# Sums of weight magnitudes moved between engines at the start of a gated block kernel, with a new order around up's mean

## The reference

```
def weight_quant(w):
    scale = 1.0 / clip(mean(abs(w)), EPS, None)
    q = clip(round(w * scale), -1.0, 1.0) / scale
def act_quant(x):
    scale = 127.0 / clip(max(abs(x), axis=-1), EPS, None)
    q = clip(round(x * scale), -128.0, 127.0) / scale
x = x + tanh(g_xattn) * mlstm(layernorm(x), ctx, ctx, ...)
y = layernorm(x)
g, u = act_quant(y) @ weight_quant(w_gate).T, act_quant(y) @ weight_quant(w_up).T
h = square(relu(g)) * u
x = x + tanh(g_ffn) * (act_quant(h) @ weight_quant(w_down).T)
```

## Time and profile before

| | |
|---|---|
| median of 3 runs | 606.54 us (606.44 to 607.38) |
| the profiled execution | 606.26 us, of it span 604.5 us |
| TensorE products busy | 579.7 us, 96% |
| VectorE busy | 529.8 us, 88% |
| ScalarE busy | 449.5 us, 74% |
| GpSimd busy | 125.8 us, 21% |
| DMA | 62.68 MB, 104 GB/s mean |

### The profile page before, as it was taken

How to read it: one execution, slowest core, us unless ns; L and a number is a source line. 1 busy time by engine, 2 the same in 40 slices (tenths; PEclk the granted TensorE clock), 3 DMA queues, 4 the chain that set the end, 5 groups by cost and what they waited for, 6 DMA issues and landing times.

```text
span 604.5 us, 18405 instructions
## 1 busy us (share of the span) xinstructions
PE 579.7 (96%) x6584; PEld 340.3 (56%) x6584; DVE 529.8 (88%) x1152; ACT 449.5 (74%) x922; POOL 125.8 (21%) x284
## 2 busy tenths in 40 slices
PE   8997779999999999999999999999999999999996
PEld 4744445656565565656565565656565565656452
DVE  3899998998989898998989898998989899897964
ACT  4789779687786868687786868687686868687662
POOL 3255052120121212020121212031121212021100
PEclk9999879999999999999999999999999999999999
DMA  8958132050504114060503205050502305030000
GB/s 304 383 199 300 46 122 72 21 193 2 195 17 142 67 38 171 3 206 0 192 17 120 90 23 186 0 209 0 188 21 91 118 18 192 3 106 1 20 36 35
DMA packets 44113, 62.68 MB, mean 104 GB/s; under 512 B 1848, under 2 KB 25648, under 8 KB 44080
## 3 DMA queue, kind: packets, MB, share of 16 engines
q1 hardware_dynamic: 44080, 62.24, 29.3%
HBM read 53.72 MB, written 8.51 MB: 103 GB/s over the span
## 4 chain that ended last, share of the span: by engine, by line
PE 77%; DVE 8%; ACT 6%; issue 5%; POOL 2%; DMA 1%; DVEq 0%; SPq 0%; ACTq 0%; POOLq 0%
PE yb L1230 16%; PE gb L1204 16%; PE ub L1204 16%; PE tp L1251 8%; PE ab L1238 7%; PE ab L1218 4%; PE tp L1278 3%; PE ab L1261 2%; PE ab L1239 2%; POOL stage L446 2%; DVE stage L806 1%; PE ab L1312 1%; ACT wgT L535 1%; ACT wdT L535 1%; DMA xs<-in_x 1%
## 5 line engine op out<-in xcount | busy, mean ns | idle before, releaser
L1204 PE MATMUL gb<-wgT,xqT 128*128 128x512 bf16 x512 | 133.5, 384 | 0.1
L1204 PE MATMUL ub<-wuT,xqT 128*128 128x512 bf16 x512 | 132.8, 382 | 0.6 <-DVE stage L806 0.5
L1230 PE MATMUL yb<-wdT,stage 128*128 128x512 bf16 x512 | 120.6, 380 | 1.8 <-ACT stage L557 1.8
L543 ACT ACTIVATE relu<-gb 128x512 f32<-128x512 f32 x128 | 75.1, 587 | 45.9 <-PE gb L1204 45.6
L806 DVE TENSOR_TENSOR stage<-relu,ub 128x512 f32<-128x512 f32 x128 | 86.8, 678 | 15.4 <-ACT relu L545 14.5
L1204 PEld LDWEIGHTS ub<-wuT,xqT 128*128 128x128 bf16 x512 | 49.7, 99 | 64.0 <-DVE stage L806 5.4
L545 ACT ACTIVATE relu<-relu 128x512 f32<-128x512 f32 x128 | 80.8, 631 | 4.1
L933 DVE SCALAR_TENSOR_TENSOR dmat<-ab,dmat 128x384 f32<-128x384 f32 x128 | 65.0, 548 | 19.0 <-POOL dmat L454 13.5
L1230 PEld LDWEIGHTS yb<-wdT,stage 128*128 128x128 bf16 x512 | 47.1, 98 | 49.9 <-ACT stage L557 1.1
L1204 PEld LDWEIGHTS gb<-wgT,xqT 128*128 128x128 bf16 x512 | 46.1, 101 | 45.1 <-issue 1.3
L454 POOL TENSOR_SCALAR_AFFINE_SELECT dmat<-dmat 128x256 f32<-128x256 f32 x128 | 55.4, 461 | 62.9 <-ACT dmat L603 50.4
(11 more groups left out here) (131 smaller groups left out, 896.4 us busy)
## 6 DMA issues: line engine op xcount, KB each, us to landing
dmat<-max_rows SPq DMA_DIRECT2D x15, 1024.0 KB, 5.0
values<-in_ctx_v SPq DMA_DIRECT2D x16, 520.0 KB, 7.6
xs<-in_x SPq DMA_DIRECT2D x16, 512.0 KB, 5.8
cT<-in_ctx_t SPq DMA_DIRECT2D x16, 512.0 KB, 6.9
out<-stage SPq DMA_DIRECT2D x32, 256.0 KB, 2.0
stage<-in_w_gate SPq DMA_DIRECT2D x4, 1024.0 KB, 12.8
stage<-in_w_up SPq DMA_DIRECT2D x4, 1024.0 KB, 13.8
stage<-in_w_down SPq DMA_DIRECT2D x4, 1024.0 KB, 7.1
```

Source lines behind the costliest of these rows:

```text
L543: nc.scalar.activation(relu[:, c % 2, :], gb[c % 2][:, :], ACT.Relu).then_inc(g_free, 1)
L1204: last = nc.tensor.matmul(bank[c % 2][:, :], xqT[par][:, t, d, :], w[:, d, c * CH:(c + 1) * CH], start=(d == 0), stop=(d == KD - 1))
L1230: done = nc.tensor.matmul(yb[:, :], hqT[:, c, :], wdT[:, c, :], start=(c == 0), stop=(c == KF - 1))
```

## The change

- The sum of piece 1 of up and that of piece 2 of down go from VectorE to ScalarE.
- The sum of piece 3 of down is made from the identity |w| = 2 max(w, 0) - w. GpSimd writes max(w, 0) of the piece into the second half of wdT (four operations of 128 x 512). TensorE multiplies the piece by a constant -4/128 and the positive part by 2 x 4/128, each as four products with 32 stationary columns and 512 moving ones, whose results go to four groups of 32 rows of yb. VectorE then sums the 512 columns of yb into asum. This adds waits: TensorE on GpSimd's four operations, VectorE on TensorE's products.
- In VectorE's prologue log_forget(1) and cumulative(1,1) go behind scale_heads and the residuals, the token statistics ahead of the running maximum, and quantise_tokens(0) ahead of weight_scale(1), the mean of up.
- GpSimd waits for the token statistics between the scalings of pieces 0 and 1 of gate.
- ScalarE takes the sum of piece 3 of up after tokens_rstd; it takes the sign of piece 1 of gate after those of piece 0 of up, and that of piece 2 in step 0 after the first relu and square.
- TensorE's keep_warm counts around weight_total(1) are 6, 5 and 8 in place of 12 and 20.

The diff, cut to its core:

```
 gpsimd
+            nc.gpsimd.memset(twice[:, :], 2 * KD / P).then_inc(positive_done, 1)
+            nc.gpsimd.memset(minus[:, :], -KD / P).then_inc(positive_done, 1)
...
             scale_weight(0, 0)
+            gp.wait_ge(ln2_step, 4)
             scale_weight(0, 1)
...
                     token_factor(0, 0)
+                    gp.wait_ge(w_in[2][3], 16)
+                    for k in range(KD):
+                        part = slice(CH * k, CH * (k + 1))
+                        nc.gpsimd.tensor_scalar(positive[:, part], weight_piece(2, 3)[:, part], 0.0, 0.0,
+                                                ALU.max, ALU.add).then_inc(positive_done, 1)
                     scale_weight(2, 0)
 scalar
-            magnitudes(1, 2, 3)
-            magnitudes(1, 3, 4)
+            magnitudes(1, 1, 3)
+            magnitudes(1, 2, 4)
             tokens_rstd(0)
+            magnitudes(1, 3, 5)
             sign_weight(0, 0)
-            sign_weight(0, 1)
-            sign_weight(1, 0)
             quantise_second(0)
             tokens(0, 0)
-            sign_weight(0, 2)
+            sign_weight(1, 0)
+            sign_weight(0, 1)
             exponentials(1, 0, 1)
...
                 relu_square(b, 0, 0)
                 if third:
+                    sign_weight(0, 2)
                     exponentials(n, 1, npar)
...
                 relu_square(b, 0, 3)
+                if third:
+                    magnitudes(2, 2, 8)
 vector
             gates_in(1)
-            magnitudes(1, 1)
-            log_forget(1)
             dve.wait_ge(tanh_done, 1)
             scale_heads(0)
-            cumulative(1, 1)
+            log_forget(1)
             residual(0, 0)
             second_residual(0, 0)
+            cumulative(1, 1)
+            token_stats(0, 0)
             dve.wait_ge(rows_spread, NP)
             running_max(1, 1)
-            token_stats(0, 0)
             token_centres(0, 0)
+            quantise_tokens(0)
             weight_scale(1)
...
             scale_weight(1, 0)
-            dve.wait_ge(winv_step, WINV[1] + 2)
-            quantise_tokens(0)
...
-                if not prev:
-                    magnitudes(2, 2)
                 hidden(b, 0, 2)
...
                 hidden_max(b, 0, 0)
+                hidden(b, 0, 3)
                 if not prev:
-                    magnitudes(2, 3)
-                hidden(b, 0, 3)
+                    dve.wait_ge(columns_done, 1)
+                    nc.vector.tensor_reduce(asum[:, 2, 3:4], yb[:, :], axis=AX_X, op=ALU.add).then_inc(asum_done[0], 1)
 tensor
+            def column_sums():
+
+                pe.wait_ge(positive_done, 2 + KD)
+                pe.wait_ge(winv_step, WSUM[1])
+                for weights, src, first in ((minus, weight_piece(2, 3), True), (twice, positive, False)):
+                    for k in range(KD):
+                        rows = slice(P // KD * k, P // KD * (k + 1))
+                        done = nc.tensor.matmul(yb[rows, :], weights[:, :], src[:, CH * k:CH * (k + 1)], start=first, stop=not first)
+                done.then_inc(columns_done, 1)
...
             max_columns(1)
-            keep_warm(12, ub[1])
+            keep_warm(6, ub[1])
             weight_total(1)
-            keep_warm(20, ub[1])
+            keep_warm(5, ub[1])
             token_columns(0)
+            keep_warm(8, ub[1])
...
                 chunk(b, 0, 3, par)
+                if not prev:
+                    column_sums()
                 if n is not None:
                     heads_out(n, 2, npar)
```

More of the change, by code:

```diff
@@ L82, in gated_block @@
         asum = sb("asum", [P, 3, 4], F32)
+        twice = sb("twice", [P, P // KD], F32)
+        minus = sb("minus", [P, P // KD], F32)
+        positive = wdT[:, :, :].rearrange("p k d -> p (k d)").bitcast(F32)[:, FF:2 * FF]
         wmean = sb("wmean", [P, 3], F32)
@@ L168, in gated_block @@
         total_done = sem("total_done")
+        positive_done = sem("positive_done")
+        columns_done = sem("columns_done")
         winv_step = sem("winv_step")
@@ L711, in step @@
                 else:
-                    magnitudes(2, 0, 5)
+                    magnitudes(2, 0, 6)
                 relu_square(b, 0, 2)
@@ L717, in step @@
                 if third:
-                    magnitudes(2, 1, 6)
+                    magnitudes(2, 1, 7)
                 relu_square(b, 0, 3)
+                if third:
+                    magnitudes(2, 2, 8)
                 if n is not None:
@@ L1180, in weight_total @@
             def weight_total(m):
-                pe.wait_ge(asum_done[0], (2, 3, 5)[m])
-                pe.wait_ge(asum_done[1], (2, 5, 7)[m])
+                pe.wait_ge(asum_done[0], (2, 2, 3)[m])
+                pe.wait_ge(asum_done[1], (2, 6, 9)[m])
                 if m > 0:
```

## The result

The changed kernel took 609.68 us (median of 5 runs, 609.35 to 609.91) against 606.54 (605.65 to 607.38): a ratio of 1.0056, 95% interval 1.004 to 1.0072. **It is slower, by 3.1 us between the medians and by 3.4 us (0.56%) by the ratio**, and outside the range of the prediction (604.5 to 607.9). The span of the profiled execution grew from 604.5 to 608.1.

The account below looks back on a forecast made before the run. TensorE, busy for 96% of the span, bounds from about 94 us; before that, down's mean on VectorE decides. The mean comes 0.4 us earlier: 606.54 - 0.4 = 606.1 us, range 604.5 to 607.9.

Parts of the forecast that it names:

- The relay and its start: Before down's mean: ScalarE's last sign of gate ends at 57.1, piece 3 lands at 62.3, GpSimd waits for it.
- GpSimd's four operations: Positive parts of down's piece 3 on GpSimd: 3.2 to 4.2 us, taken as 3.65, ending at 66.0.
- The column sums: TensorE's products for down's piece 3: 1.9 us at full clock, 3.6 at half, the 32-wide groups overlapping.
- The slower rival: TensorE's column groups do not overlap: C 72.8 and 610.1 us in series, 608.4 overlapped in twos; chance 0.14.
- C: End of TensorE's column_sums: 67.9 at full clock, 69.6 at half, mostly near 68.8.
- The clock: TensorE, idle 2 to 3.6 us before column_sums, runs most of it at 1.2 GHz: 3.6 us.
- C + 6.7: Down's mean is ready 6.7 us after C, through heads_out and VectorE's normaliser; break-even is C = 69.2.
- The sum: With C = 68.8, down's mean comes 0.4 us earlier, near 75.5.
- Step 1, 18.5 us behind the mean: Step 1 starts 18.5 us after down's mean, over GpSimd and ScalarE work the edit leaves alone.
- The shift is carried one for one: From about 94 us TensorE's repeated steps bound; time won or lost before is carried unchanged to the end.
- The prologue: ScalarE stays the bound, its queue 0.5 us earlier; VectorE's first weigh some 2.2 us earlier; GpSimd's new wait covered.
- it waits some 2 us, and that is where its 3.9 us go: VectorE, 3.9 us ahead by losing two sums, reaches its wait for column_sums at 66.9 and loses the lead there.

Follow-up runs that it names:

- Experiments 1 and 2: First: changed kernel, GpSimd's maximum replaced by multiply-add, 603.55 us. Second: changed kernel with GpSimd operations added at its quiet end; maximum-add 1.89 us, multiply-add 0.59.
- experiment 1: Changed kernel with GpSimd's four operations as multiply and add instead of maximum and add (mean only approximate): 603.55 us against 605.26, ratio 0.9971.
- experiment 4: Changed kernel with unused TensorE products ahead of column_sums: ten gave 609.93 us, ratio 1.0062; eighteen gave 608.01 us, ratio 1.0045.
- the sums alone: Changed kernel with the old prologue, keeping the new way for down's sums: 610.89 us, ratio 1.009 to the kernel before.
- the prologue alone: Changed kernel with down's sums as before (VectorE takes pieces 2 and 3), keeping the new prologue: 602.27 us against 605.26, ratio 0.9951.
- experiment 3: Half of the change each, against the kernel before: new prologue with old down sums 602.27 us, ratio 0.9951; new sums with old prologue 610.89 us, ratio 1.009.

## Why the prediction was wrong

- *The relay and its start.* The last sign of gate was to end at 57.1 and ended at 56.94; the load was to land at 62.3 and landed at 62.04. GpSimd waited for it, as said.
- *The step that failed: GpSimd's four operations at 3.2 to 4.2 us, taken as 3.65.* They took 7.75. I bounded an operation that the trace did not have (a maximum) by the nearest rows (multiply and add), and took the spread of those rows, which I put down to contention, for the whole uncertainty. No row said that another arithmetic operation has the same price. Experiments 1 and 2 put the price on the operation: 1.89 against 0.59 in quiet. By this term alone the end of the positive parts moved from 66.0 to 69.9. The upper bound of that cost was wrong, so the range was too. The rows didn't even bound a multiply-add with constants: four took 2.54 in experiment 1, below the 3.2.
- *The column sums.* 1.9 us at full clock and 3.6 at half were right: 1.85 (experiment 1), 1.86 (experiment 4) and 3.50. The 32-wide groups do overlap: 16 instructions in series would be 6.8. The slower rival named that as its mechanism and was wrong on it, though its break-even on C (69.2) fits. Its figures (C 72.8, 610.1 us) lie near the measured ones by luck.
- *The clock.* "Mostly near 68.8" for C had set about half the clock's cost, and all of it was paid: 0.7 us more. The reason given for it does not hold as it stands. It let chunk (0,0,3) end at 62.4 to 64 and a wait of 2 to 3.6 us lower the clock. The clock was already at 0.50 when the chunk began, and the chunk ended at 65.5, so with GpSimd through at 66.0 only 0.5 us of wait would have been left. In experiment 1, where column_sums followed without a wait, the clock rose from 64 to 65 and all of them had the full clock; in the changed kernel TensorE stopped at 65.5, and the clock stayed at 0.50 over the 4.4 us. So this cost, too, came with the late GpSimd; what the clock does after a wait of 0.5 us no run shows.
- *C + 6.7.* C was 73.42, the mean 80.11: 6.7. In experiment 1, 66.91 and 73.60: 6.7 again. Here the rows carried. It takes heads_out at full clock: where heads_out(1,2) ran at half clock (the sums alone, and ten unused products) it was 7.3.
- *The sum.* Forecast for the mean 75.5; the late GpSimd adds 3.9 and the clock 0.7: 80.1, as measured. VectorE waited 6.25 us where 2 were forecast.
- *Step 1, 18.5 us behind the mean.* It began at 98.91, 18.8 behind. But here the mean isn't what it waits for: from 76.28 the chain goes over ScalarE's copy of the heads, the queries' transposes and the next chunk, to a scaling on VectorE at 89.72 and a sign on ScalarE at 90.95, and passes down's mean and GpSimd's scalings by. This road hangs on the same late heads_out, so both were late together. With the prologue alone the chain does pass through the mean (73.03, step 1 at 91.54, 18.5).
- *The shift is carried one for one.* Nearly. Step 1's first store is issued 4.5 us later (95.77 and 100.28), the last group of stores 3.6 later (541.52 and 545.09). With the prologue alone the lead of 3.1 (92.63) grows to 4.15. The changed kernel, the prologue alone and experiment 1 all gain 0.6 to 1 us on the kernel before somewhere in the middle, the first two mostly in steps 1 to 4. What does this was not sought and stays open; it is also why the span grew by 3.6 us and not by 4.2 or more.
- *The prologue.* ScalarE as its bound, 0.5 us ahead (0.7 in the profile, of it 0.2 from an earlier start), GpSimd's wait covered, VectorE 2 us ahead at its first weigh (49.14 against 51.24): as said. That half would have been a forecast of 604.4, and experiment 3 gave 0.9951, which is 603.6 of 606.5.
- *What I did not ask:* what the change would be without its weakest part. VectorE stood for 6.25 us in order to save 2.27, less the 0.69 of its new reduction. The prediction had the sentence ("it waits some 2 us, and that is where its 3.9 us go") and did not draw from it that the plain sum in that gap costs less than the relay.

## What to carry to other kernels

When work is moved to another engine, the operation is priced by a row of that same operation on that engine, and not by a row of the same shape. Where there is none, the bound must allow a factor, not a spread: here 1.9 to 2.4 against the rows taken, and 3.2 between two operations of one form. And a sum that is taken from the bound engine must not come back to it as a wait: if the moved work depends on the latest load and passes through three engines, its length has to be set against the gap that the bound engine has anyway.

## What the runs showed of the hardware

- GpSimd on 128x512 float32, nothing else at work: multiply-add 0.59 us, an add of two tiles 1.01, anything with a maximum or minimum 1.46 to 1.90. "GPSIMD Engine Reference" of the Trainium skill (section "4.1 Engine selection") has add, multiply and maximum in one line, with operations of one input roughly at line rate. The runs part multiply-add and maximum-add by a factor of 3.2, and the measurement decides.
- "GPSIMD Engine Reference" of the Trainium skill (section "3.1 Elementwise — side-by-side cycle accounting") gives 2.6 cycles per element for an operation with two inputs. The same section of the Trainium skill has 1.03 cycles for the shortest loop bodies and, for a tight unrolled loop, a best case of 1.8, which is 769 ns for 512 elements. The runs agree in the order of two inputs and one (1.01 us against 0.59), and the multiply-add is below the 769 ns. The 1.89 us of a maximum with one input is above even the two-input add, which goes against this order.
- Four groups of 32 columns with float32 moving data of 512 columns overlap fully: 16 instructions in 1.85 us at 2.4 GHz (experiment 1) and 3.50 at 1.2 GHz (the changed kernel).
- The clock changed in the middle of a run of equal products (experiment 4: eight in 0.89 us, the next eight in 1.88).
- The last 16 down products stand behind the same idle time in all twelve traces (1.3 us ahead of a group of transposes, and 0.8 between these and the products). In nine they took 3.61 us, in three 5.30: there the clock fell, which alone makes 1.7 us.
